# A decoder layer: another home for batch 1's x, another tile for batch 0's wkv, and new instruction lists

## The chip, the cores and the metric

The kernel runs on one core of a Trainium2 chip. A core has five engines with their own instruction streams: TensorE (PE, matmuls; PEld is its weight load), VectorE (DVE), ScalarE (ACT), GpSimd (POOL) and SyncE (SP), which here issues every DMA. Engines meet only at semaphores. The metric is the device time of one execution in microseconds, the median of several runs. All data is float32, 128 rows (partitions) at a time.

## What is computed

x and ctx are (4, 512, 512): four batches of 512 tokens with 512 channels. The reference, cut:

```python
x = x + attn(layernorm(x))
x = x + wkv2(w, u, k=layernorm(x), v=ctx)
x = x + ffn(layernorm(x))

def attn(x):                       # RWKV-4 time mix
    xs = x shifted by one token
    k, v, r = (x*tm + xs*(1-tm)) @ W.T     # three projections, each its own tm and W
    wkv = scan over tokens: (e1*aa + e2*v) / (e1*bb + e2), with a running maximum
    return (sigmoid(r) * layernorm(wkv) * g + b ...) @ Wo.T
def ffn(x):                        # 1408 inner channels
    return ((silu(x @ G.T * gs) * (x @ U.T * us)) @ Dn.T) * ds
```

wkv2 is a scan of the same kind without projections. Both scans run along the tokens and carry their state, channel by channel.

## The kernel before

Each batch passes through a row of steps. A step is a short piece of one engine's stream, named by kind, index and batch ("up6.0" is unit 6 of batch 0). The order in which an engine takes its steps is written out by hand in five lists of the file, PE_STEPS, ACT_STEPS, DVE_STEPS, POOL_STEPS and SP_STEPS; nothing else sets it, and every engine takes its own steps strictly in turn. Each step waits at semaphores for what it needs.

For one batch: x is loaded (xload), DVE takes its statistics (stat1), DVE and ACT normalise it (norm0, norm1), PE transposes it so that channels lie on partitions (turn1). ACT copies it scaled (share_k, share_v, share_r), DVE adds the shifted part (mixk, mixv, mixr), and PE projects (k, v, r: four units each of four 512-wide matmuls). The first scan is done by DVE and ACT per group of 128 channels: front, den, nv, num, part, fin; fin writes wkv. PE turns wkv back to tokens (turn2), its statistics are taken (stat2), it is normalised (norm2, norm3), turned again (return2), scaled and gated (rw, with the tanh of r), and projected (wo). x1 adds the first residual (loaded by rload into xres) and x's sums are taken for the next layernorm (sq on ACT, nb and rn on POOL, norm4, norm5). turn3, the second scan (xfront, xin, xden, xnum, xpart, xfin), y (turn back), xf (second residual), norm6, norm7, turn4_0 and turn4_1 (the two halves of the tokens), z4 (split in a high part z4h by ACT and a rest z4l by DVE). The FFN has 22 up units (sixteen 256-wide matmuls each, one 128-channel slice of one half of the tokens), for each a silu and a prod that make h, its split (high, rest), and 22 down units of four 512-wide matmuls. out writes the result.

The projections and the turns of all batches share four PSUM banks in turn: use n of a bank waits until use n-4 has been read (need_drained). The two slots of the scans are shared likewise. The FFN of batch b runs on PE beside the attention of batch b+1, which mostly DVE and ACT work on.

Tiles that matter here: mixv holds x of a batch from its load on, then v's mixed input. xres holds the first residual, xf the second. zt holds the transposed, normalised x; `wkv = zt` (L265) has the first scan write into it when x is no longer wanted. So share_k0 of batch b waits for turn2 of batch b-1 (L739), and load_x of batch 1 (L422) waits until the last nv of batch 0 has read v. load_res (L428) for batch 0 stands in the head of the SP stream, ahead of the FFN's weights. mixr of batch 0 is in z, of batch 1 in xf, then in mixk. There is a step kind "warm" (L638) for two 128x128 matmuls of the identity into a PSUM tile that nobody reads; the list before doesn't use it.

Of the kernel before, what the change touches and what calls it, by code (L numbers as in the profile page):

```python
# [44 lines left out]
def decoder_layer(nc, x, ctx_t, wk_t, wv_t, wr_t, wo_t, vecs_in, gate_t, up_t, down_t, ffn_scales, down_s, out):  # L45
# [21 lines left out]
    def steps(text):  # L67
# [8 lines left out]
        up15.0 up16.0 up17.0 down11.0 up18.0 r1.2 down12.0 down13.0 up19.0 down14.0 up20.0 up21.0
        down15.0 down16.0 down17.0 r2.2 down18.0 down19.0 down20.0 down21.0 y.1 r3.2 turn4_0.1 turn4_1.1
        up0.1 turn2.2 up1.1 up2.1 up3.1 return2.2 up4.1 down0.1 down1.1 turn1.3 up5.1 wo.2 k0.3 k1.3
        v0.3 v1.3 k2.3 k3.3 up6.1 up7.1 down2.1 v2.3 v3.3 down3.1 down4.1 up8.1 up9.1 turn3.2 down5.1
        up10.1 up11.1 down6.1 down7.1 up12.1 up13.1 down8.1 down9.1 down10.1 up14.1 up15.1 r0.3 up16.1  # L80
        up17.1 down11.1 r1.3 r2.3 r3.3 down12.1 up18.1 up19.1 down13.1 down14.1 down15.1 y.2 up20.1
        down16.1 down17.1 up21.1 down18.1 turn4_0.2 down19.1 down20.1 down21.1 up0.2 up1.2 up2.2 up3.2
        turn4_1.2 up4.2 turn2.3 up5.2 up6.2 down0.2 down1.2 return2.3 up7.2 wo.3 up8.2 up9.2 turn3.3
        down2.2 down3.2 up10.2 down4.2 down5.2 up11.2 down6.2 down7.2 up12.2 up13.2 down8.2 down9.2
        down10.2 up14.2 up15.2 up16.2 up17.2 down11.2 down12.2 down13.2 up18.2 down14.2 down15.2 up19.2
# [18 lines left out]
        share_v0.2 silu6.0 share_v1.2 share_v2.2 share_v3.2 sq4.1 norm4.1 sq5.1 norm5.1 front0.2
        front1.2 part0.2 share_r0.2 share_r1.2 silu7.0 part1.2 high2.0 high3.0 share_r2.2 front2.2
        silu8.0 silu9.0 front3.2 share_r3.2 silu10.0 silu11.0 part2.2 part3.2 high4.0 high5.0 silu12.0
        silu13.0 high6.0 xfront0.1 xfront1.1 silu14.0 silu15.0 tanh0.2 silu16.0 silu17.0 xpart0.1
        xpart1.1 xfront2.1 high7.0 silu18.0 high8.0 silu19.0 xfront3.1 silu20.0 silu21.0 xpart2.1
# [1016 lines left out]
```

## Time and profile before

| | us |
|---|---|
| median of 3 runs | 588.87 (588.06 to 589.04) |
| profiled execution | 589.12 |
| its span, first to last instruction | 587.2 |
| PE busy | 531.2 (90%) |
| DVE busy | 458.0 (78%) |
| ACT busy | 361.9 (62%) |
| mean granted clock of PE | 0.972 |

The profile is one execution. A timeline row gives the start in us, the length in us, the engine, the line of the kernel, the operation with out<-in, the shapes, the count of instructions merged in the row and, in brackets, how long the engine had been idle before it and what ended that.
### The profile page before, as it was taken

To read this page: it belongs to the slowest core of one execution; us is meant where nothing else is said; L and a number is where in the kernel's file an instruction comes from. 1 tells how busy PE (TensorE), PEld (TensorE's weight loads), DVE (VectorE), ACT (ScalarE), POOL (GpSimd) and SP (SyncE) were. 2 spreads that over 40 slices of the span, in tenths; PEclk is the share of its full clock that TensorE was granted. 3 is DMA by queue.
4 is the path that set the end of the run, shared out by engine and by line. 5 is a ranking of instruction groups with operands and counts; after the bars stand their busy time and mean duration, and the time that the engine had idled before them with its cause. 6 is when DMAs were issued, how large, how long until landed. Compare 5 with 4: busy or idle time off the path is not lost.

```text
span 587.2 us, 7506 instructions
## 1 busy us (share of the span) xinstructions
PE 531.2 (90%) x2658; PEld 379.4 (65%) x2658; DVE 458.0 (78%) x742; ACT 361.9 (62%) x559; POOL 51.0 (9%) x155
## 2 busy tenths in 40 slices
PE   1899388769589999999979999999999999999995
PEld 1444244324288447888658446985989588999995
DVE  4899878799987689999966699999867289853344
ACT  2828789655748458767757466887645377743321
POOL 2000300200222100000023110000101100101000
PEclk9999899889869999999999999999999999999999
DMA  8999800010220000010340000001120010000011
GB/s 308 413 300 390 326 0 0 2 36 0 76 104 2 0 1 0 2 37 1 116 136 1 0 1 0 2 31 60 55 73 2 0 37 28 9 19 19 1 37 38
DMA packets 14263, 39.08 MB, mean 67 GB/s; under 512 B 1232, under 2 KB 1232, under 8 KB 14032
## 3 DMA queue, kind: packets, MB, share of 16 engines
q1 hardware_dynamic: 14224, 38.57, 18.9%
q8 instruction: 23, 0.38, 0.3%
q14 instruction: 16, 0.13, 0.1%
HBM read 34.37 MB, written 12.85 MB: 80 GB/s over the span
## 4 chain that ended last, share of the span: by engine, by line
PE 62%; DVE 19%; ACT 7%; issue 7%; POOL 4%; DMA 1%; SPq 0%; POOLq 0%; DVEq 0%; ACTq 0%
PE gu L658 23%; PE bank L570 12%; PE dacc L584 12%; PE bank L632 9%; PE bank L559 5%; DVE t_slot L885 2%; ACT L681 2%; DVE t_slot L945 1%; DVE t_st L1023 1%; POOL t_rstd L532 1%; DVE t_stats L911 1%; DVE t_slot L966 1%; DVE t_stats L864 1%; DVE t_slot L949 1%; ACT t_mixk L712 1%
## 5 line engine op out<-in xcount | busy, mean ns | idle before, releaser
L658 PE MATMUL gu<-t_z4h,t_gate 128*128 128x256 f32 x352 | 91.9, 294 | 3.6 <-DVE t_h L1060 1.4
L658 PE MATMUL gu<-t_z4h,t_up 128*128 128x256 f32 x352 | 87.9, 283 | 0.0
L658 PE MATMUL gu<-t_z4l,t_up 128*128 128x256 f32 x352 | 87.9, 282 | 0.0
L658 PE MATMUL gu<-t_z4l,t_gate 128*128 128x256 f32 x352 | 87.8, 282 | 0.0
L810 ACT ACTIVATE t_h<-gu,t_fsc 128x256 f32<-128x256 f32 x88 | 40.7, 472 | 64.4 <-PE gu L658 55.2
L681 ACT ACT_TABLE_LOAD x60 | 77.0, 1283 | 1.8 <-PEq L1119 0.7
L1060 DVE SCALAR_TENSOR_TENSOR t_h<-gu,t_fsc,t_h 128x256 f32<-128x256 f32 x88 | 41.1, 478 | 40.2 <-ACT t_h L810 40.1
L658 PEld LDWEIGHTS gu<-t_z4h,t_gate 128*128 128x128 f32 x352 | 66.8, 190 | 8.2 <-DVE t_h L1060 3.0
L584 PE MATMUL dacc<-t_down,t_hh 128*128 128x512 f32 x176 | 71.1, 404 | 0.2
L584 PE MATMUL dacc<-t_down,t_hl 128*128 128x512 f32 x176 | 68.9, 391 | 0.0
L658 PEld LDWEIGHTS gu<-t_z4l,t_gate 128*128 128x128 f32 x352 | 66.9, 190 | 2.2 <-issue 1.4
L658 PEld LDWEIGHTS gu<-t_z4l,t_up 128*128 128x128 f32 x352 | 66.9, 190 | 0.0
L658 PEld LDWEIGHTS gu<-t_z4h,t_up 128*128 128x128 f32 x352 | 66.9, 190 | 0.0
L570 PE MATMUL bank<-t_mixk,t_wk 128*128 128x512 f32 x128 | 59.4, 614 | 3.0 <-DVE t_mixk L894 3.0
L570 PE MATMUL bank<-t_mixv,t_wv 128*128 128x512 f32 x128 | 56.8, 593 | 0.9 <-ACT t_z L784 0.9
L632 PE MATMUL bank<-t_wo,t_tanh_r 128*128 128x512 f32 x128 | 55.6, 592 | 0.0
L570 PEld LDWEIGHTS bank<-t_mixk,t_wk 128*128 128x128 f32 x128 | 24.7, 196 | 35.6 <-issue 30.0
L570 PEld LDWEIGHTS bank<-t_mixv,t_wv 128*128 128x128 f32 x128 | 24.2, 190 | 30.4 <-issue 28.9
L632 PEld LDWEIGHTS bank<-t_wo,t_tanh_r 128*128 128x128 f32 x128 | 24.1, 190 | 29.2 <-issue 27.5
L695 ACT ACTIVATE t_hh<-t_h 128x512 fp32r<-128x512 f32 x44 | 27.2, 625 | 21.4 <-PE dacc L584 11.6
L885 DVE TENSOR_TENSOR t_slot<-t_slot 128x1024 f32<-128x1024 f32 x32 | 39.0, 1218 | 0.7 <-ACT t_slot L797 0.7
L904 DVE TENSOR_TENSOR t_hl<-t_h,t_hh 128x512 fp32r<-128x512 f32 x44 | 29.7, 684 | 12.0 <-ACT t_hh L695 11.8
(128 smaller groups left out, 924.9 us busy)
## 6 DMA issues: line engine op xcount, KB each, us to landing
t_mixv<-in_x SPq DMA_DIRECT2D x8, 512.0 KB, 4.9
t_xres<-in_x SPq DMA_DIRECT2D x8, 512.0 KB, 4.4
t_ctxt<-in_ctx_t SPq DMA_DIRECT2D x16, 256.0 KB, 2.7
out<-t_otile SPq DMA_DIRECT2D x16, 256.0 KB, 2.4
...
```

The source lines that it names most:

```text
L532: pool.tensor_tensor(rstd[:, half(k)], veps[:, half(k)], small[:, MINUS_HALF, half(k)], ALU.pow).then_inc(rstd_done, 1)
L559: done = pe.transpose(bank_of(b, s, m)[:, k * P:(k + 1) * P], src[:, k, m * P:(m + 1) * P], ident[:, :])
L570: last = pe.matmul(bank_of(b, s, c)[:, :], w[:, k, c * P:(c + 1) * P], src[:, k, :], start=(k == 0), stop=(k == C - 1))
L584: last = pe.matmul(dacc[j][:, :], as_read(part[:, ring(b, u), j * P:(j + 1) * P], exact), as_read(down[:, i, :], exact), start=(i == 0 and ...
L632: done = pe.matmul(bank_of(b, s, m)[:, :], tanh_r[:, k, m * P:(m + 1) * P], wo[:, k, :], start=(k == 0), stop=(k == C - 1))
L658: last = pe.matmul(gu[u % 2][:, side, :], as_read(w[:, k, i * P:(i + 1) * P], exact), as_read(part[:, k, hf * HALF:(hf + 1) * HALF], exact ...
L681: act.preload_act_table_set(name)
L695: act.activation(pair(hh, b, p), pair(h, b, p), ACT.Copy).then_inc(hh_done, 1)
L810: act.activation(h[:, ring(b, u), :], gu[u % 2][:, 0, :], ACT.Silu, scale=fsc[:, 0, u % NI:u % NI + 1]).then_inc(silu_done, 1)
L885: dve.tensor_tensor(slot[:, c % 2, 2:4, :], both, slot[:, c % 2, 0:1, :].to_broadcast([P, 2, T]), ALU.mult).then_inc(square, 1)
L904: dve.tensor_tensor(pair(hl, b, p), pair(h, b, p), pair(hh, b, p).bitcast(F32), ALU.subtract).then_inc(hl_done, 1)
L1060: dve.scalar_tensor_tensor(out=h[:, ring(b, u), :], in0=gu[u % 2][:, 1, :], scalar=fsc[:, 1, u % NI:u % NI + 1], in1=h[:, ring(b, u), :], ...
```

## The change

1. x of batch 1 is loaded in the head of the program, where the first residual of batch 0 was loaded, into xf instead of mixv. Its statistics and the reads of norm0 and norm1 of batch 1 go to xf; they still write mixv, now after v of batch 0 is projected.
2. The first residual of batch 0 is loaded later, after turn2 of batch 0, since xres now holds wkv of batch 0 until then.
3. share_k0 waits for what still reads its target tiles, batch by batch, no longer always for turn2 of the batch before.
4. All five lists are new. PE's has 26 "warm" steps, all in batch 0.

```diff
-        wkv = zt
+        def wkv(b):
+            return xres if b == 0 else zt
+        def x_home(b):
+            return xf if b == 1 else mixv
...
             def load_x(b, hf):
-                need(sp, newv_done, b - 1, C)
-                sp.dma_start(mixv[:, hf * HB:(hf + 1) * HB, :], rows_of(b, hf)).then_inc(x_in[hf], 16)
+                if b > 1:
+                    need(sp, newv_done, b - 1, C)
+                sp.dma_start(x_home(b)[:, hf * HB:(hf + 1) * HB, :], rows_of(b, hf)).then_inc(x_in[hf], 16)
             def load_res(b, hf):
+                if b == 0:
+                    need_filled(sp, 0, "turn2", TB - 1)
                 need(sp, xf_done, b - 1, (hf + 1) * HB)
...
-            load_res(0, 0)
-            load_res(0, 1)
+            load_x(1, 0)
+            load_x(1, 1)
...
                     if c == 0:
-                        need(act, tanh_done, b - 1, C)
-                        need_before(act, b, "turn2", C - 1)
+                        if b > 0 and mixr(b - 1) is mixk:
+                            need(act, tanh_done, b - 1, C)
+                        elif b > 0:
+                            need_filled(act, b - 1, "k", C - 1)
+                        if b > 0 and wkv(b - 1) is zt:
+                            need_filled(act, b - 1, "turn2", C - 1)
+                        else:
+                            need(act, mix_done, b - 1, 3 * C)
...
     PE_STEPS = steps("""
-        turn1.0 k0.0 k1.0 v0.0 v1.0 k2.0 k3.0 r0.0 r1.0 v2.0 v3.0 r2.0 r3.0 turn2.0 turn1.1 k0.1 k1.1
+        warm0.0 warm1.0 warm2.0 warm3.0 warm4.0 warm5.0 turn1.0 warm6.0 warm7.0 warm8.0 k0.0 k1.0 v0.0
```

In DVE's list the steps of batch 0's scan are in another order in the head (front0.0 stands ahead of mixv3.0 and mixr0.0), rw0 to rw2 of batch 0 stand between front0.1 and mixv2.1, and stat1_0.1 and stat1_1.1 stand where they stood, behind stat2_0.0 and stat2_1.0.

PE, from turn2 of batch 0 (the second transposes that read t_zt or t_xres) to wo.0 (t_wo). Before, from turn2.0:

```order
L559 MATMUL bank<-t_ident,t_zt 128x128 x16
L559 MATMUL bank<-t_ident,t_mixv 128x128 x16
L570 MATMUL bank<-t_mixk,t_wk 128x512 x8
L570 MATMUL bank<-t_mixv,t_wv 128x512 x4
L559 MATMUL bank<-t_ident,t_z 128x128 x16
L570 MATMUL bank<-t_mixv,t_wv 128x512 x4
L632 MATMUL bank<-t_wo,t_tanh_r 128x512 x16
```

Now, from the two warm steps ahead of turn2.0 (gu<-t_ident):

```order
L650 MATMUL gu<-t_ident 128x128 x4
L568 MATMUL bank<-t_ident,t_xres 128x128 x16
L650 MATMUL gu<-t_ident 128x128 x4
L568 MATMUL bank<-t_ident,t_mixv 128x128 x16
L579 MATMUL bank<-t_mixk,t_wk 128x512 x4
L650 MATMUL gu<-t_ident 128x128 x12
L568 MATMUL bank<-t_ident,t_z 128x128 x16
L579 MATMUL bank<-t_mixk,t_wk 128x512 x4
L579 MATMUL bank<-t_mixv,t_wv 128x512 x8
L650 MATMUL gu<-t_ident 128x128 x2
L641 MATMUL bank<-t_wo,t_tanh_r 128x512 x16
```

return2.0 (the transposes of t_z) moved from behind k0.1, k1.1 and v0.1 to behind k0.1 alone, with six warm steps ahead of it; k1.1, v0.1 and v1.1 stand between it and wo.0, and two more warm steps stand ahead of turn1.1.

DVE, around batch 0's last layernorm, from part2.1 (before) and from xf_0.0 (now). t_xf,t_sums is xf, t_z4l is the rest part of the FFN's input, the pair on t_slot 128x1024 and t_zt is fin2.1, t_slot<-t_slot,t_st is part. Before:

```order
L977 TENSOR_TENSOR t_slot<-t_slot,t_st 128x2x512
L1048 SCALAR_TENSOR_TENSOR t_xf,t_sums<-bank,t_xres 128x512 x3
L1074 TENSOR_SCALAR t_general<-gu 1x1
L1048 SCALAR_TENSOR_TENSOR t_xf,t_sums<-bank,t_xres 128x512
L959 SCALAR_TENSOR_TENSOR t_st<-t_fade,t_slot 128x512
L972 SCALAR_TENSOR_TENSOR t_st<-t_fade,t_slot 128x512
L877 TENSOR_SCALAR t_z<-t_xf,t_rstd,t_nmr 128x512
L977 TENSOR_TENSOR t_slot<-t_slot,t_st 128x2x512
L877 TENSOR_SCALAR t_z<-t_xf,t_rstd,t_nmr 128x512
L885 TENSOR_TENSOR t_slot<-t_slot 128x1024
L887 SCALAR_TENSOR_TENSOR t_zt<-t_slot 128x512
L1055 TENSOR_TENSOR t_z4l<-bank,t_z4h 128x2x256 x4
```

Now:

```order
L1067 SCALAR_TENSOR_TENSOR t_xf,t_sums<-bank,t_xres 128x512 x4
L1086 TENSOR_REDUCE t_inexact<-t_low_sums 128x1
L996 TENSOR_TENSOR t_slot<-t_slot,t_st 128x2x512
L978 SCALAR_TENSOR_TENSOR t_st<-t_fade,t_slot 128x512
L1093 TENSOR_SCALAR t_general<-gu 1x1
L894 TENSOR_SCALAR t_z<-t_xf,t_rstd,t_nmr 128x512
L991 SCALAR_TENSOR_TENSOR t_st<-t_fade,t_slot 128x512
L894 TENSOR_SCALAR t_z<-t_xf,t_rstd,t_nmr 128x512
L996 TENSOR_TENSOR t_slot<-t_slot,t_st 128x2x512
L1074 TENSOR_TENSOR t_z4l<-bank,t_z4h 128x2x256 x2
L902 TENSOR_TENSOR t_slot<-t_slot 128x1024
L904 SCALAR_TENSOR_TENSOR t_zt<-t_slot 128x512
```

The first half of z4l moved ahead of fin2.1 and behind part3.1; part2.1 stands behind xf, where before it stood ahead of xf.

PE, around y.1 (bank<-t_ident,t_z 128x128 behind the last down unit of batch 0); t_wr with t_mixk is r3.2. Before:

```order
L584 MATMUL dacc<-t_down,t_hh 128x512
L584 MATMUL dacc<-t_down,t_hl 128x512
L559 MATMUL bank<-t_ident,t_z 128x128 x16
L570 MATMUL bank<-t_mixk,t_wr 128x512 x4
L609 MATMUL bank<-t_ident,t_z 128x128 x16
L658 MATMUL gu<-t_z4h,t_gate 128x256
```

Now:

```order
L593 MATMUL dacc<-t_down,t_hh 128x512
L593 MATMUL dacc<-t_down,t_hl 128x512
L568 MATMUL bank<-t_ident,t_z 128x128 x16
L618 MATMUL bank<-t_ident,t_z 128x128 x16
L667 MATMUL gu<-t_z4h,t_gate 128x256
L667 MATMUL gu<-t_z4l,t_gate 128x256
```

r3.2 stands no longer between y.1 and turn4 of batch 1; it moved ahead of the last four down units of batch 0.

## Rows read from the trace of the kernel before

**Rows 1.** Windows of all engines: length, busy (instructions) by engine, clock, DMA, GB/s
```profile
0.00:167.10 167.10, 123.45 (x339) 61.30 (x339) 141.75 (x223) 111.38 (x161) 17.25 (x55) 0.92 0.48 172
167.10:188.30 21.20, 21.02 (x161) 20.79 (x162) 16.69 (x39) 13.29 (x23) 5.55 (x16) 0.89 0.01 2
202.00:292.70 90.70, 90.44 (x449) 64.65 (x447) 84.61 (x116) 64.84 (x91) 1.62 (x7) 1.00 0.08 24
292.70:302.50 9.80, 6.12 (x25) 3.17 (x25) 6.07 (x15) 6.95 (x15) 2.93 (x10) 1.00 0.71 215
302.50:581.40 278.90, 276.45 (x1656) 223.45 (x1656) 198.44 (x334) 158.61 (x258) 22.45 (x64) 1.00 0.06 20
```

**Rows 2.** Windows of PE alone: length, busy, granted clock, DMA
```profile
68.00:70.00 2.00, 0.00 (x0) 0.79 1.06 389
76.00:78.00 2.00, 0.70 (x2) 1.00 0.00 0
126.00:128.00 2.00, 0.00 (x0) 0.80 0.00 0
156.00:158.00 2.00, 0.00 (x0) 0.98 0.23 10
170.00:172.00 2.00, 2.00 (x13) 0.61 0.00 0
```

**Rows 3.** Windows of DVE alone
```profile
16.00:63.30 47.30, 45.21 (x56) 1.00 1.01 371
```

**Rows 4.** Timeline of PE, 10 to 64 us: start, us, line, operation
```profile
53.69 7.03 PE L570 MATMUL bank<-t_z,t_wr 128*128 128x512 f32 x16
62.90 1.31 PE L559 MATMUL bank<-t_ident,t_zt 128*128 128x128 f32 x10 [1.85 <-ACT t_tanh_r L759]
```

**Rows 5.** Part 6 of the page, the loads of x
```profile
t_mixv<-in_x SPq DMA_DIRECT2D x8, 512.0 KB, 4.9
```

**Rows 6.** Timeline of the DMA queue
```profile
56.04 1.08 SPq L426 DMA_DIRECT2D t_mixv<-in_x  x2
```

**Rows 7.** Timeline of all engines, 60 to 77 us
```profile
64.25 1.29 DVE L864 BATCH_NORM_STATS2 t_stats<-bank 128x6 f32<-128x512 f32 x2 [1.01 <-PE bank L559]
67.21 1.25 DVE L911 BATCH_NORM_STATS2 t_stats<-t_mixv 128x6 f32<-128x512 f32 x2
72.13 3.67 PE L559 MATMUL bank<-t_ident,t_mixv 128*128 128x128 f32 x16 [7.59 <-DVE t_mixv L919]
```

**Rows 8.** Timeline of PE, 76 to 99 us
```profile
77.30 7.66 PE L570 MATMUL bank<-t_mixk,t_wk 128*128 128x512 f32 x16 [1.50 <-DVE t_mixk L894]
89.91 1.64 PE L559 MATMUL bank<-t_ident,t_z 128*128 128x128 f32 x13 [1.18 <-DVE t_slot L966]
95.95 3.60 PE L632 MATMUL bank<-t_wo,t_tanh_r 128*128 128x512 f32 x8
```

**Rows 9.** Timeline of DVE, 107 to 186 us
```profile
154.32 1.23 DVE L977 TENSOR_TENSOR t_slot<-t_slot,t_st 128x1024 f32<-128x1024 f32 x1
163.81 1.22 DVE L885 TENSOR_TENSOR t_slot<-t_slot 128x1024 f32<-128x1024 f32 x1
165.67 2.47 DVE L1055 TENSOR_TENSOR t_z4l<-bank,t_z4h 128x512 fp32r<-128x512 f32 x4
```

**Rows 10.** Timeline of PE, 110 to 168 us
```profile
129.37 2.93 PE L570 MATMUL bank<-t_xf,t_wr 128*128 128x512 f32 x3 [5.17 <-DVE t_slot L1005]
162.18 3.74 PE L609 MATMUL bank<-t_ident,t_z 128*128 128x128 f32 x16 [7.23 <-DVE t_z L877]
167.10 0.55 PE L658 MATMUL gu<-t_z4h,t_gate 128*128 128x256 f32 x1 [1.18 <-DVE t_z4l L1055]
```

**Rows 11.** Timeline of PE, 278 to 306 us
```profile
291.04 1.64 PE L559 MATMUL bank<-t_ident,t_z 128*128 128x128 f32 x13 [0.19 <-ACT t_tanh_r L759]
293.21 3.70 PE L570 MATMUL bank<-t_mixk,t_wr 128*128 128x512 f32 x8 [0.53 <-DVE t_xf L1048]
298.63 1.40 PE L609 MATMUL bank<-t_ident,t_z 128*128 128x128 f32 x8 [1.72 <-DVE t_z L877]
```

More of the change, by code:

```diff
@@ L76, in decoder_layer @@
[L76 to L85, printed above, removed]
@@ new lines, in decoder_layer @@
+        v1.0 k2.0 k3.0 v2.0 v3.0 r0.0 r1.0 r2.0 r3.0 warm9.0 warm10.0 turn2.0 warm17.0 warm18.0 turn1.1
+        k0.1 warm11.0 warm12.0 warm13.0 warm14.0 warm15.0 warm16.0 return2.0 k1.1 v0.1 v1.1 warm19.0
+        wo.0 warm20.0 warm21.0 turn3.0 r0.1 r1.1 r2.1 r3.1 k2.1 k3.1 v2.1 v3.1 warm22.0 warm23.0 y.0
+        flag.0 warm24.0 warm25.0 turn4_0.0 turn4_1.0 up0.0 up1.0 turn2.1 up2.0 up3.0 up4.0 down0.0
+        return2.1 up5.0 down1.0 up6.0 turn1.2 up7.0 wo.1 k0.2 k1.2 v0.2 k2.2 k3.2 up8.0 up9.0 v1.2 v2.2
@@ new lines, in decoder_layer @@
+        up10.0 down2.0 up11.0 down3.0 down4.0 down5.0 v3.2 down6.0 down7.0 down8.0 down9.0 up12.0 up13.0
+        turn3.1 up14.0 down10.0 up15.0 r0.2 up16.0 r1.2 down11.0 up17.0 down12.0 down13.0 up18.0 up19.0
+        down14.0 down15.0 down16.0 down17.0 up20.0 up21.0 r2.2 r3.2 down18.0 down19.0 down20.0 down21.0
+        y.1 turn4_0.1 turn4_1.1 up0.1 turn2.2 up1.1 up2.1 up3.1 return2.2 down0.1 down1.1 up4.1 turn1.3
+        up5.1 wo.2 k0.3 k1.3 v0.3 v1.3 k2.3 k3.3 v2.3 up6.1 up7.1 down2.1 down3.1 down4.1 down5.1 v3.3
@@ L104, in decoder_layer @@
[L104 to L108, printed above, removed]
@@ L130, in decoder_layer @@
         stat1_0.0 stat1_1.0 norm0.0 norm1.0 mixk0.0 mixk1.0 mixk2.0 mixk3.0 mixv0.0 mixv1.0 mixv2.0
-        mixv3.0 mixr0.0 front0.0 front1.0 mixr1.0 den0.0 nv0.0 mixr2.0 num0.0 nv1.0 part0.0 den1.0
-        num1.0 part1.0 fin0.0 mixr3.0 fin1.0 front2.0 front3.0 den2.0 nv2.0 num2.0 part2.0 nv3.0 den3.0
-        num3.0 part3.0 fin2.0 fin3.0 stat2_0.0 stat2_1.0 stat1_0.1 stat1_1.1 norm2.0 norm3.0 norm0.1
-        norm1.1 mixk0.1 mixk1.1 mixk2.1 mixk3.1 mixv0.1 mixv1.1 mixv2.1 mixv3.1 front0.1 front1.1 nv0.1
@@ new lines, in decoder_layer @@
+        part3.0 fin2.0 fin3.0 stat2_0.0 stat2_1.0 stat1_0.1 stat1_1.1 norm2.0 norm3.0 norm0.1 norm1.1
+        mixk0.1 mixk1.1 mixk2.1 mixk3.1 mixv0.1 mixv1.1 front0.1 rw0.0 rw1.0 rw2.0 mixv2.1 mixv3.1 rw3.0
+        mixr0.1 front1.1 nv0.1 den0.1 nv1.1 num0.1 part0.1 den1.1 num1.1 mixr1.1 part1.1 x1_0.0 x1_1.0
+        x1_2.0 fin0.1 x1_3.0 norm4.0 fin1.1 norm5.0 mixr2.1 mixr3.1 xfront0.0 xfront1.0 xin0.0 xin1.0
+        xden0.0 xnum0.0 xpart0.0 xden1.0 xnum1.0 xpart1.0 xfin0.0 xfront2.0 xfin1.0 xin2.0 xfront3.0
@@ new lines, in decoder_layer @@
+        mixk2.2 prod6.0 prod7.0 x1_3.1 mixk3.2 mixv0.2 mixv1.2 mixv2.2 mixv3.2 front0.2 front1.2 den0.2
+        nv0.2 num0.2 part0.2 norm4.1 norm5.1 den1.2 mixr0.2 mixr1.2 mixr2.2 fin0.2 prod8.0 front2.2
+        nv1.2 num1.2 part1.2 prod9.0 nv2.2 fin1.2 front3.2 den2.2 rest3.0 rest4.0 num2.2 part2.2
+        prod10.0 prod11.0 nv3.2 rest5.0 den3.2 num3.2 part3.2 prod12.0 prod13.0 fin2.2 mixr3.2 fin3.2
+        xfront0.1 rest6.0 out0.0 xfront1.1 xin0.1 prod14.0 prod15.0 xden0.1 xnum0.1 xpart0.1 xin1.1
@@ new lines, in decoder_layer @@
+        rw3.2 x1_0.2 mixk1.3 mixk2.3 mixk3.3 mixv0.3 mixv1.3 mixv2.3 mixv3.3 rest1.1 x1_1.2 x1_2.2
+        front0.3 prod4.1 x1_3.2 front1.3 den0.3 nv0.3 num0.3 prod5.1 part0.3 den1.3 norm4.2 norm5.2
+        nv1.3 rest2.1 num1.3 part1.3 mixr0.3 fin0.3 mixr1.3 fin1.3 front2.3 front3.3 den2.3 prod6.1
+        prod7.1 nv2.3 num2.3 nv3.3 prod8.1 part2.3 prod9.1 rest3.1 den3.3 num3.3 prod10.1 prod11.1
+        part3.3 rest4.1 mixr2.3 fin2.3 mixr3.3 fin3.3 xfront0.2 rest5.1 prod12.1 prod13.1 xfront1.2
```

168 lines of the change are left out of this document (84 added, 84 removed).

## Prediction

> **What bounds the kernel now.** I read the windows of all engines first, then the clock of TensorE (PE) where it waits, then the timelines around the waits.
>
> The windows cut the span in two parts [rows 1]. Up to 167.10 us, where the first FFN unit starts (up0.0), PE is busy 123.45 us of 167.10 and VectorE (DVE) 141.75: this part is a chain, mostly of DVE work, in which PE waits and in places runs slowly (mean granted clock 0.92). From 167.10 on PE is the bound: 21.02 of 21.20, 90.44 of 90.70 and, at the end, 276.45 of 278.90 us busy. Between these lies one hole, 292.70 to 302.50, where PE is busy 6.12 of 9.80 us: batch 1's second residual, its layernorm and turn4 have to pass before up0.1 can run. The reader is to see two rules in this. Before 167 us a shorter chain is a gain; after it, a PE unit taken out of the hole and put in front of it costs its full length.
>
> Where PE waits, its granted clock falls to the lower of its two levels. After the wait before turn1.1 it fell at about 69.2 us (0.79 is the mean of 68 to 70) and was back by 76.0; after the others it fell at about 127.2, then at about 157.9, and in this last case returned only at about 171.6 (0.61 over 170 to 172 is 1.56 us at half) [rows 2]. The waits were 7.59, 5.17 and 7.23 us [rows 7, 10]; 1.85 us of waiting before turn2.0 cost no clock [rows 4].
>
> **The change part by part.** My milestones are the start of wo.0, of up0.0, the end of y.1, the start of up0.1, and the end.
>
> The early load of x. Before, x of batch 1 is issued at 56.04 us and takes 4.9 us to land, some 61 us [rows 5, 6]. Its first reader, stat1_0.1, starts at 67.21 [rows 7], right behind stat2 of batch 0, and the new list of DVE leaves it there. The load was hidden, so its move is worth 0. It takes the place of the first residual's load, of the same size; that residual now waits for turn2.0 (some 64 us) and is wanted by x1_0.0 only after wo.0 has begun, at 95.95 [rows 8], over 30 us later: 0, and 4.9 us could go wrong without harm. wkv in the other tile costs the same writes and reads: 0. It frees zt for batch 1, but PE still has turn2.0 ahead of turn1.1, so nothing is released by it.
>
> The head, to batch 0's stats. DVE is busy 45.21 of 47.30 us from 16.0 to 63.3 [rows 3]; the new list holds the same operations, so at most 2.1 us go and at least 0. Putting front0.0 ahead of mixv3.0 and mixr0.0 and spreading the waits should take about half of it. The tanh on ScalarE (ACT) that frees the last bank of turn2.0 (the 1.85 us wait of rows 4) comes about as much earlier. I take -1.0 us for the stats at 64.25 and, with them, turn1.1 at 72.13 [rows 7].
>
> The warm-up matmuls. 26 steps of two 128x128 matmuls go into the waits of batch 0. Four matmuls of 128x512 take 7.03 - 3.60 = 3.43 us (x16 against x8) [rows 4, 8], so one takes 0.86, a 128-wide one a quarter of that, 0.21 us, and a step of two 0.43 us at full clock and 0.86 at half. They lie in waits except six steps behind k0.1 (2.6 us) and one before wo.0 (0.4 us). The two steps ahead of turn1.1 run at once behind turn2.0; over 6 us of waiting remain, near the three waits that did lose the clock, so turn1.1 and the start of k0.1 run at half. Before, the clock came back at 76.0, ahead of k0.1 at 77.30 [rows 2, 8]. After other restarts it took longer: from r2.1 at 129.37 about 4.7 us, from turn4 at 162.18 about 9.4 us [rows 2, 10]. I take 4.7 from k0.1's start (77.30 - 1.0 = 76.3): 4.7 us at half do 2.35 of its 3.43, the other 1.1 run at full, and it ends at 82.1. Before it took 7.66 - 3.60 = 4.06 us, paced by its inputs [rows 8], which would end it at 80.4. The ends are 0 and +3.4 us (all of k0.1 slow); I take +1.7.
>
> wo.0. PE goes on in a row: six warm-ups 2.6, return2.0 1.8, k1.1, v0.1 and v1.1 10.3, a warm-up 0.4: 82.1 + 15.1 = 97.2, against 95.95 [rows 8]. So +1.25 us, from -0.5 to +2.9. What waits behind it is x1, the layernorm and xfront0.0. Before, return2.0 stood later, at 89.91, after a wait of 1.18 us [rows 8]; the six warm-ups now sit where it would otherwise start.
>
> From wo.0 to up0.0. DVE is saturated in most of it. One partial sum (part2.1, at 154.32, 1.23 us) goes from ahead of batch 0's xf to behind it [rows 9]; the warm-ups behind wo.0 may shorten turn3.0 by some 0.4. So xf is at 1.25 - 1.2 - 0.4, about -0.3. Then the new list puts z4l of the first half ahead of fin2.1, which took 163.81 to 165.67 [rows 9]. up0.0 waited for it 1.18 us after turn4, which ended at 162.18 + 3.74 = 165.92 [rows 10]. Now it can start as turn4 ends, so at most 1.18 us go; part3.1 lands ahead of z4l, so I take 0.9 and get **up0.0 at -1.2 us**, 165.9; ends -3.0 and +0.8.
>
> From up0.0 to y.1. PE does the same units as before plus one: r3.2 stood behind y.1 (293.21, 3.70 us with its drain) [rows 11] and now stands ahead of it, 3.43 us. PE had no room for it: its idle time in 167.10 to 188.30 and in 202 to 292.70 is 0.18 and 0.26 us [rows 1]. I count +3.43, less these 0.44: +3.0, and y.1 ends at 292.68 - 1.2 + 3.0 = 294.5. The ends are +2.5 and +5 (the other moves of ups and downs, each of which must find its h ready).
>
> From y.1 to up0.1. This is a chain of DVE, ACT and POOL, 9.8 us before [rows 1], and I leave it at that. What r3.2 hid there is now an idle PE: from 292.68 to 298.63 is 5.95 us [rows 11], between the waits of 5.17 and 7.59 that lost the clock. There is no warm-up step in it. In batch 0 the low clock reached 4.46 us past up0.0's start (171.56 - 167.10), which is 2.2 us lost [rows 2, 10]. That row is the nearest case: +2.2, ends 0 and 3.4.
>
> The Trainium skill (TensorE: Matmul & The Clock Gate, "What's actually happening") says that the gate's monitor is free-running and not reset by the kernel's start. It would make each of these clock terms differ from run to run by its phase; the executions before, 588.06 to 589.04, are compatible with that and show no more.
>
> After up0.1 the same 159 PE steps follow in a slightly different order over 278.90 us with 2.45 us idle [rows 1]: 0, ends -2.4 and +2.4.
>
> **Sum.** -1.2 + 3.0 + 0 + 2.2 + 0 = +4.0 us on the profiled execution's 589.12, 593.1. That execution stood 0.25 above the median of 588.87, so 592.9.
>
> **The rivals.**
> The clock is held. If the warm-ups keep PE at its upper level through batch 0, k0.1 is 1.7 us earlier and turn4 and up0.0 lose nothing (2.2 us less): 592.9 - 3.9 = 589.0, no change. For it: 26 steps, two of them just ahead of turn4. Against: the waits are longer than the pairs. If the clock also stays up behind y.1, 2.2 more go and the kernel is **faster**, 586.8. It decides where the granted clock between 155 and 172 us, and between 294 and 310, stands at the lower level for less than about 1 us.
>
> The FFN of batch 0 finds its inputs late. PE has no slack after 167, so each wait that the moved downs, k3.2 and v2.2 make adds itself; two waits of 1.5 us give 595.9. For it: DVE too is nearly full there (84.61 of 90.70 us) [rows 1]. Against: only small moves.
>
> The change does nothing of weight: x's load was hidden, and 3.0 us ahead of y.1 could be met by a head better than I think (up0.0 at -3.0 instead of -1.2) and the 2.45 us of late idle time. That gives 592.9 - 1.8 - 2.2 = 588.9 as well.
>
> **How the numbers follow.** The forecast (591.0 to 594.6) gets 0.46, the late inputs 0.12, the held clock without the second stretch 0.12, with it 0.16, the last rival 0.09, the rest 0.05 to either side. 0.2% (1.2 us) is about what a measurement of this kernel can tell from no change. The two cases at 589 (0.21) I split 0.07 faster, 0.12 same, 0.02 slower. So faster 0.07 + 0.16 + 0.02 = 0.25, same 0.13, slower 0.62. The range 586.5 to 595.8 leaves out less than one in ten on either side; the forecast's own is 591.0 to 594.6.
>
> **What would show it.** In the changed profile: wo.0's first matmul near 97, up0.0 near 166, y.1 ending near 294.5, up0.1 near 304; between y.1 and turn4_0.1 no PE work for about 6 us, and a granted clock at half for a stretch that begins there; from up0.1 to PE's last matmul 279 to 281 us. The prediction is wrong if y.1 ends before 292.7, if up0.0 stands before 164, or if the clock stays up behind y.1.

## The result, and the profile after

The changed kernel takes 592.84 us (median of 4 executions, 592.11 to 593.17) against 588.87: the ratio is 1.0062, with a 95% interval of 1.0041 to 1.0083. It is slower by some 4 us. The forecast was 592.9 us. The profiled execution took 593.17 us, with a span of 591.4 us and a mean granted clock of 0.964.

The windows of all engines of the changed kernel, cut at the same events as [rows 1] (columns as there):

```profile
0.00:167.90 167.90, 135.46 (x442) 74.73 (x442) 139.74 (x220) 103.95 (x154) 18.52 (x55) 0.90 0.48 171
167.90:191.10 23.20, 23.04 (x184) 22.65 (x185) 18.82 (x42) 14.40 (x25) 5.15 (x16) 0.97 0.01 2
204.80:294.70 89.90, 89.86 (x433) 62.97 (x431) 86.48 (x119) 64.50 (x90) 4.27 (x8) 1.00 0.09 27
294.70:304.50 9.80, 3.73 (x17) 3.19 (x17) 5.95 (x14) 6.08 (x14) 2.92 (x10) 0.73 0.61 188
304.50:585.50 281.00, 277.19 (x1656) 223.69 (x1656) 198.83 (x333) 153.07 (x255) 20.61 (x64) 1.00 0.06 20
```

Three things are to be seen against [rows 1]. The hole between y.1 and up0.1 is again 9.80 us long, but PE is busy 3.73 us in it and no longer 6.12: r3.2 has gone from it. The last stretch has the same 1656 PE instructions, but PE idles 3.81 us in it, where it idled 2.45. And the mean clock ahead of up0.0 is 0.90, not 0.92, in spite of the warm steps.

The timeline of PE in the changed kernel, in the head, around y.1 and around y.2 (start and length in us, line; L568 turns, L579 projects, L618 is turn4, L667 an up unit, L593 a down unit, L641 wo):

```profile
71.28 3.68 PE L568 MATMUL bank<-t_ident,t_mixv 128*128 128x128 f32 x16 [6.70 <-DVE t_mixv L938]
76.46 5.81 PE L579 MATMUL bank<-t_mixk,t_wk 128*128 128x512 f32 x8 [1.50 <-DVE t_mixk L911]
84.78 1.91 PE L568 MATMUL bank<-t_ident,t_z 128*128 128x128 f32 x16
87.56 3.70 PE L579 MATMUL bank<-t_mixk,t_wk 128*128 128x512 f32 x8 [0.87 <-ACT t_z L801]
98.41 1.88 PE L641 MATMUL bank<-t_wo,t_tanh_r 128*128 128x512 f32 x4
...
163.94 3.68 PE L618 MATMUL bank<-t_ident,t_z 128*128 128x128 f32 x16 [2.85 <-DVE t_z L894]
168.06 0.55 PE L667 MATMUL gu<-t_z4h,t_gate 128*128 128x256 f32 x1 [0.45 <-DVE t_z4l L1074]
...
282.23 7.03 PE L579 MATMUL bank<-t_mixk,t_wr 128*128 128x512 f32 x16
292.76 1.91 PE L568 MATMUL bank<-t_ident,t_z 128*128 128x128 f32 x16
300.62 3.71 PE L618 MATMUL bank<-t_ident,t_z 128*128 128x128 f32 x16 [5.96 <-DVE t_z L894]
304.48 0.55 PE L667 MATMUL gu<-t_z4h,t_gate 128*128 128x256 f32 x1
...
423.97 0.66 PE L568 MATMUL bank<-t_ident,t_z 128*128 128x128 f32 x4 [0.50 <-DVE t_z L904]
425.83 0.66 PE L568 MATMUL bank<-t_ident,t_z 128*128 128x128 f32 x4 [1.20 <-DVE t_z L904]
432.52 1.09 PE L618 MATMUL bank<-t_ident,t_z 128*128 128x128 f32 x8 [0.47 <-DVE t_z L894]
```

These rows answer to [rows 7, 8, 10 and 11]. wo.0 stands at 98.41 (before 95.95), up0.0 at 168.06 (167.10), y.1 ends at 292.76 + 1.91 = 294.67 (292.68), up0.1 stands at 304.48 (302.49). The last three rows are y.2 and turn4_0.2; their waits, 2.17 us in all, have no counterpart before.

The granted clock of PE in the changed kernel (2 us each: busy, clock, DMA):

```profile
68.00:70.00 2.00, 0.00 (x0) 0.50 1.03 380
168.00:170.00 2.00, 1.94 (x11) 0.62 0.05 12
304.00:306.00 2.00, 1.85 (x9) 0.50 0.06 17
306.00:308.00 2.00, 2.00 (x19) 0.99 0.00 0
```

It is at the lower level up to about 169.5 us behind up0.0, 1.5 us of running at half where [rows 2] had 4.46; and up to 306.0 behind up0.1, 1.5 us again, where before it was never low.

**An account that adds up.** For each profile I cut the time from up0.0 on in three: up0.0 to the end of y.1 (the middle), the hole up to up0.1, and up0.1 to PE's last matmul (the late stretch). From the middle and the late stretch I take off what the clock cost: PE's busy time times (1 - granted clock), summed over windows of 1 us. What is left, the net length, repeats within 0.4 us between profiles whose lists are the same there; the clock's part differs from execution to execution. The last row of the table is the sum for this pair of profiles.

| us | up0.0 | middle, net | clock | hole | late, net | clock | last matmul |
|---|---|---|---|---|---|---|---|
| before | 167.10 | 123.35 | 2.23 | 9.81 | 278.85 | 0.00 | 581.34 |
| changed | 168.06 | 125.88 | 0.73 | 9.81 | 280.35 | 0.78 | 585.61 |
| difference | +0.96 | +2.53 | -1.50 | 0 | +1.50 | +0.78 | +4.27 |

### The profile page after: what moved, and what is told of

Its sections match the earlier page's. It is cut to its first block, busy times and chain, and to the rows that moved or that the text cites. A ratio compares the mean times of both kernels' runs of the same rounds, so it can differ in the third digit from the quotient of the medians.

```text
span 591.4 us, 7709 instructions
## 1 busy us (share of the span) xinstructions
PE 543.1 (92%) x2762; PEld 393.3 (67%) x2762; DVE 458.3 (77%) x742; ACT 350.2 (59%) x551; POOL 51.8 (9%) x155
## 4 chain that ended last, share of the span: by engine, by line
PE 83%; DVE 8%; ACT 3%; issue 3%; POOL 2%; DMA 1%; SPq 0%; POOLq 0%; DVEq 0%; ACTq 0%
PE gu L667 27%; PE bank L579 26%; PE dacc L593 13%; PE bank L641 9%; PE bank L568 6%; PE bank L618 1%; ACT L690 1%; DVE t_stats L928 1%; DVE t_otile L1100 1%; PE gu L650 1%; DMA t_vecs<-in_vecs 1%; DVE t_slot L902 1%; DVE t_st L1042 1%; DVE t_z L894 1%; DVE t_xf L1067 1%
## 5 line engine op out<-in xcount | busy, mean ns | idle before, releaser
L667 PE MATMUL gu<-t_z4h,t_gate 128*128 128x256 f32 x352 | 92.9, 297 | 1.3 <-DVE t_h L1079 0.7
L667 PE MATMUL gu<-t_z4l,t_gate 128*128 128x256 f32 x352 | 88.2, 283 | 0.0
L667 PE MATMUL gu<-t_z4l,t_up 128*128 128x256 f32 x352 | 87.3, 281 | 0.0
L667 PE MATMUL gu<-t_z4h,t_up 128*128 128x256 f32 x352 | 87.2, 281 | 0.0
L667 PEld LDWEIGHTS gu<-t_z4h,t_gate 128*128 128x128 f32 x352 | 67.3, 191 | 6.7 <-issue 3.2
L593 PE MATMUL dacc<-t_down,t_hh 128*128 128x512 f32 x176 | 71.0, 403 | 0.8 <-DVE t_otile L1100 0.7
L593 PE MATMUL dacc<-t_down,t_hl 128*128 128x512 f32 x176 | 68.9, 391 | 0.0
L667 PEld LDWEIGHTS gu<-t_z4l,t_gate 128*128 128x128 f32 x352 | 67.2, 191 | 2.5 <-issue 1.7
L667 PEld LDWEIGHTS gu<-t_z4h,t_up 128*128 128x128 f32 x352 | 66.4, 189 | 0.0
L667 PEld LDWEIGHTS gu<-t_z4l,t_up 128*128 128x128 f32 x352 | 66.3, 188 | 0.0
L579 PE MATMUL bank<-t_mixk,t_wk 128*128 128x512 f32 x128 | 59.3, 615 | 2.4 <-DVE t_mixk L911 1.5
L579 PE MATMUL bank<-t_mixv,t_wv 128*128 128x512 f32 x128 | 56.6, 592 | 0.0
L641 PE MATMUL bank<-t_wo,t_tanh_r 128*128 128x512 f32 x128 | 55.6, 592 | 0.0
L579 PEld LDWEIGHTS bank<-t_mixk,t_wk 128*128 128x128 f32 x128 | 24.6, 196 | 34.3 <-issue 28.1
L579 PEld LDWEIGHTS bank<-t_mixv,t_wv 128*128 128x128 f32 x128 | 24.2, 190 | 29.3 <-issue 28.9
L641 PEld LDWEIGHTS bank<-t_wo,t_tanh_r 128*128 128x128 f32 x128 | 24.0, 190 | 28.7 <-issue 27.7
```

Source lines behind the costliest of these rows:

```text
L579: last = pe.matmul(bank_of(b, s, c)[:, :], w[:, k, c * P:(c + 1) * P], src[:, k, :], start=(k == 0), stop=(k == C - 1))
L593: last = pe.matmul(dacc[j][:, :], as_read(part[:, ring(b, u), j * P:(j + 1) * P], exact), as_read(down[:, i, :], exact), start=(i == 0 and ...
L641: done = pe.matmul(bank_of(b, s, m)[:, :], tanh_r[:, k, m * P:(m + 1) * P], wo[:, k, :], start=(k == 0), stop=(k == C - 1))
L667: last = pe.matmul(gu[u % 2][:, side, :], as_read(w[:, k, i * P:(i + 1) * P], exact), as_read(part[:, k, hf * HALF:(hf + 1) * HALF], exact ...
```

## The experiments

Each has its own comparison with the kernel before on the same chip. Lists are cut at up0.0 and up0.1 (on ACT at silu0.0 and silu0.1, on DVE at prod0.0 and prod0.1) into head, middle and late.

### 1. The new code under the old lists

```diff
-SP: copy2.0 words1.0 xload0.1 xload1.1 words2.0 ctx2.0
+SP: copy2.0 words1.0 words2.0 rload0.0 rload1.0 ctx2.0
 PE, ACT, DVE, POOL: the lists of before
```

> The new code (x of batch 1 early, wkv of batch 0 in the other tile, the later load of the first residual) with the step lists of the kernel before. Theory: the load was hidden, so 588.9 us, within 1.2 of the kernel before. Rival (the tiles or the moved loads cost something by themselves): more than 590.1.

Measured: 589.23 against 588.76 us, ratio 1.0010 (0.9995 to 1.0025). The other homes of x and of wkv, the earlier load and share_k's other waits are worth nothing that can be measured (at most 1.5 us by the interval). The 4 us, or all but a small part of them, lie in the lists.

### 2. The new head alone

```diff
-PE, ACT, DVE up to up0.0: the lists of before
+PE, ACT, DVE up to up0.0: the lists of the changed kernel, warm steps included
```

> As the run with the new code alone, but the PE, ACT and DVE lists up to the first FFN unit (up0.0, silu0.0, prod0.0) are those of the changed kernel, warm-up steps included; everything behind is as before. Theory from the two traces: up0.0 comes 1.0 us later, but the low clock ends 1.5 us instead of 4.5 us behind it, so 588.4 to 589.9, no change. Rival (the head is what costs): 591 or more.

Measured: 589.76, ratio 1.0019 (1.0005 to 1.0033). In the profile up0.0 stands at 166.28, 0.8 earlier than before. But the old lists behind it then wait: PE idles 1.33 us in the middle (before 0.41), of it 0.27 and 0.66 at turn2.1, whose input DVE now writes behind z4l. Net middle 124.97.

### 3. The new middle alone

```diff
-PE, ACT, DVE from up0.0 to up0.1; POOL; SP: the lists of before
+PE, ACT, DVE from up0.0 to up0.1; POOL; SP: the lists of the changed kernel
```

> As the run with the new code alone, but the lists between up0.0 and up0.1 (with the POOL and SP lists) are those of the changed kernel, r3.2 ahead of y.1 among them. Theory: r3.2 costs its 3.4 us less some 0.3 of waits, and the low clock behind y.1 0.8 to 2.2 us: 592 to 594. Rival (r3.2 is met by slack elsewhere and the loss is in the other parts): 590.1 or less.

Measured: 594.26, ratio 1.0097 (1.0075 to 1.0120), more than the whole change. The net middle is 125.70. The rest is an artifact of the mixture, seen in the timeline of PE:

```profile
475.30 1.09 PE L566 MATMUL bank<-t_ident,t_z 128*128 128x128 f32 x8 [1.32 <-DVE t_z L892]
477.58 1.09 PE L566 MATMUL bank<-t_ident,t_z 128*128 128x128 f32 x8 [1.19 <-DVE t_z L892]
```

POOL's new order has nb5.3 ahead of rn4.3; under the old late lists nb5.3's input comes late, and batch 3's layernorm with it: 2.5 us. Experiment 9 repeats the middle without that.

### 4. The new late stretch alone

```diff
-PE, ACT, DVE from up0.1 on: the lists of before
+PE, ACT, DVE from up0.1 on: the lists of the changed kernel
```

> As the run with the new code alone, but the lists from up0.1 on are those of the changed kernel. Theory: in the trace of the changed kernel PE was idle 3.8 us of this stretch against 2.45 before, so +1.4 us: 590.2. Rival (that idle time belongs to what comes before it): 588.9.

Measured: 591.77, ratio 1.0044 (1.0026 to 1.0062). The net late stretch is 280.25, as in the changed kernel, with PE idle for 3.85 us. The prediction had 0 for it. And r3.2 stands behind y.1 here, yet the clock fell (windows of PE):

```profile
300.00:310.00 10.00, 9.39 (x56) 0.66 0.02 7
```

That cost 2.6 us in this execution. So r3.2 in the hole does not protect the clock. The median is 1.6 us above the 590.2 expected, and the clock goes with that: the seven executions with a mean granted clock of 0.971 to 0.977 have a median of 590.38 us, the five with 0.964 to 0.966 one of 593.19.

### 5. r3.2 put back behind y.1

```diff
-PE: r2.2 r3.2 down18.0 down19.0 down20.0 down21.0 y.1 turn4_0.1
+PE: r2.2 down18.0 down19.0 down20.0 down21.0 y.1 r3.2 turn4_0.1
-ACT: tanh3.2 sq6.1 sq7.1
+ACT: sq6.1 sq7.1 tanh3.2
```

> The changed kernel with one PE step moved: r3.2 stands behind y.1 again, as in the kernel before, and its tanh on ACT behind sq7.1. Theory (r3.2 ahead of y.1 costs its full length, behind y.1 it lies in a wait): y.1 ends about 3.4 us earlier, 291.2 in place of 294.7, y.1 to up0.1 stays 9.8 us, up0.1 near 301.1, and the time is about 3.4 us below the changed kernel's 592.8, near 589.4. If the clock also stays up behind y.1, another 0.8 us. Rival (the place of r3.2 is of no weight, since what is saved ahead of y.1 comes back as late waits of the last 280 us): 592 to 593, with up0.1 earlier by 3 us and PE idle behind up0.1 longer by as much.

Measured: 593.80 (591.26 to 594.34), ratio 1.0062 (1.0040 to 1.0083), the very ratio of the changed kernel. My theory of 3.4 us fell. The timeline of PE shows where they went:

```profile
286.53 0.47 PE L593 MATMUL dacc<-t_down,t_hh 128*128 128x512 f32 x1 [1.46 <-DVE t_hl L921]
293.89 3.70 PE L579 MATMUL bank<-t_mixk,t_wr 128*128 128x512 f32 x8 [0.90 <-DVE t_xf L1067]
```

and that of DVE, which has no gap from 284.50 to 292:

```profile
284.50 1.23 DVE L1042 TENSOR_TENSOR_SCAN t_st<-t_keep,t_slot 128x512 f32<-128x512 f32 x1
285.64 0.14 DVE L1045 COPY t_st<-t_slot 128x2 f32<-128x2 f32 x1
285.69 0.69 DVE L921 TENSOR_TENSOR t_hl<-t_h,t_hh 128x512 fp32r<-128x512 f32 x1
286.30 1.28 DVE L1050 SCALAR_TENSOR_TENSOR t_slot<-t_slot,t_beta,t_st 128x1024 f32<-128x1024 f32 x1
...
291.21 0.69 DVE L904 SCALAR_TENSOR_TENSOR t_z<-t_slot 128x512 f32<-128x512 f32 x1
```

PE, rid of r3.2, waits 1.46 us for the rest (t_hl) of h that down18.0 reads, which DVE writes behind a scan, and then for the z of y.1, written at 291.9. The net middle shrinks by 0.9 only, to 124.99; the hole is 0.4 us longer (10.17), which leaves a gain of 0.5 us, less than the intervals can tell. This profile also lost 2.60 us to the clock in its late stretch, the changed kernel's 0.78. In the new lists PE and DVE are both near full there (DVE 86.48 of 89.90 us), and r3.2 is partly the filling of waits.

### 6. r3.2 ahead of y.1 in the old lists

```diff
-PE: r2.2 down18.0 down19.0 down20.0 down21.0 y.1 r3.2 turn4_0.1
+PE: r2.2 r3.2 down18.0 down19.0 down20.0 down21.0 y.1 turn4_0.1
-ACT: sq6.1 sq7.1 tanh3.2
+ACT: tanh3.2 sq6.1 sq7.1
```

> The kernel before with one PE step moved: r3.2 stands behind r2.2, far ahead of y.1, and its tanh on ACT ahead of sq6.1. Theory: y.1 ends 3.0 to 3.4 us later, up0.1 likewise, and the time is 588.9 + 3.2 = 592.1; with a low clock behind y.1 that r3.2 no longer covers, up to 2 us more (594). Rival (PE's order there costs nothing by itself, it was the other new steps of the middle that cost): 588.9 to 589.5.

Measured: 591.70, ratio 1.0039 (1.0023 to 1.0054), 2.2 us slower. Net middle 126.25 against 123.35, +2.9, near its length of 3.43 us less the 0.4 of idle time (of which 0.2 is still there); hole 9.81 and net late stretch 278.83 unchanged; the clock cost nothing behind up0.1. In the old lists, where DVE is less late, the step does cost its length.

### 7. The changed kernel without warm steps

```diff
-PE: warm0.0 ... warm25.0 (26 steps)
```

> The changed kernel without its 26 warm steps. Theory (too short to hold the clock; where they stand behind k0.1 they cost their length): behind k0.1 six steps of 0.43 us go and one ahead of wo.0, so wo.0 stands up to 3 us earlier, less what return2.0 and k1.1 wait for their inputs; some of it is DVE's chain and doesn't come through: up0.0 at 0 to -1.5 us and a time of 591.3 to 592.8. Rival (the warm steps hold the clock in part of batch 0): the clock is at half for longer at k0.1 and around turn4_0.0, up0.0 1 to 2 us later, a time of 594 to 595.

Measured: 592.12, ratio 1.0051 (1.0032 to 1.0069), 0.7 us below the changed kernel if anything; the intervals overlap. In the profile wo.0 stands at 96.84 (98.41) and up0.0 at 166.55 (168.06). The timeline of PE from k0.1 to k1.1:

```profile
76.38 5.51 PE L577 MATMUL bank<-t_mixk,t_wk 128*128 128x512 f32 x8 [1.81 <-DVE t_mixk L909]
81.72 0.49 PE L566 MATMUL bank<-t_ident,t_z 128*128 128x128 f32 x3
83.92 1.64 PE L566 MATMUL bank<-t_ident,t_z 128*128 128x128 f32 x13 [1.71 <-DVE t_slot L966]
86.43 3.70 PE L577 MATMUL bank<-t_mixk,t_wk 128*128 128x512 f32 x8 [0.87 <-ACT t_z L799]
```

They don't hold the clock: with them turn1.1 takes 3.67 to 3.68 us (changed, experiments 2, 5 and 12), without them 3.30, where 16 transposes at the upper level take 1.91. k0.1's length is a draw: 5.81, 4.23, 5.06 and 4.23 us in those four profiles, 5.51 here. From k0.1's end to wo.0 it is 16.14 to 16.15 us in all four, and 14.95 without the steps: there they cost 1.2 us. Of the six behind k0.1 (2.6 us), 1.7 us lay in a wait of return2.0 for its input; k1.1 comes 1.1 us earlier without them.

### 8. The long waits filled

```diff
-PE: turn2.0 turn1.1 ... r1.1 r2.1 ... y.0 turn4_0.0
+PE: turn2.0 (14 warm) turn1.1 ... r1.1 (9 warm) r2.1 ... y.0 (14 warm) turn4_0.0
```

(in the kernel before)

> The kernel before with 37 warm steps that fill the three long waits of batch 0 nearly whole: 14 ahead of turn1.1 (6.0 of 7.59 us), 9 ahead of r2.1 (3.9 of 5.17), 14 ahead of turn4_0.0 (6.0 of 7.23). Theory (the clock falls where PE waits for 5 us and more; work that fills the wait keeps it up): granted clock 1.00 from 20 to 290 us, r2.1 1.2 us shorter at least, turn4_0.0 1.8 us in place of 3.7, no slow stretch behind up0.0 (2.2 us): up0.0 about 2 to 3 us earlier, and the time 588.9 - 4 = 585 (at most 0.5 us back where the warm steps overrun the wait). Rival (the low clock lies off the path, since DVE sets most of it, or the clock falls all the same): 588 to 589.

Measured: 589.18, ratio 0.9998 (0.9985 to 1.0011): no change, and yet the clock did what the theory wanted. The windows of PE at the places of [rows 2] where it had fallen:

```profile
68.00:70.00 2.00, 2.00 (x20) 1.00 1.05 386
128.00:130.00 2.00, 2.00 (x20) 1.00 0.03 8
156.00:158.00 2.00, 2.00 (x20) 1.00 0.00 0
168.00:170.00 2.00, 2.00 (x20) 1.00 0.02 4
```

turn4 of batch 0 takes two pieces of 1.09 us where it took 3.74. But the timeline of PE shows what its speed is worth:

```profile
162.54 1.09 PE L613 MATMUL bank<-t_ident,t_z 128*128 128x128 f32 x8 [0.98 <-DVE t_z L881]
164.31 1.09 PE L613 MATMUL bank<-t_ident,t_z 128*128 128x128 f32 x8 [0.68 <-DVE t_z L881]
167.46 0.36 PE L662 MATMUL gu<-t_z4h,t_gate 128*128 128x256 f32 x1 [2.05 <-DVE t_z4l L1059]
```

up0.0 now waits 2.05 us for z4l, behind fin2.1 on DVE, and stands where it stands with the old head unfilled (167.48 in the mean of seven profiles). In the old head the low clock ahead of up0.0 lies off the path.

### 9. The new middle again, with POOL and SP as before

```diff
-POOL: nb4.3 nb5.3 rn4.3 rn5.3
+POOL: nb4.3 rn4.3 nb5.3 rn5.3
```

(against experiment 3; nb5.1 likewise behind rn4.1, and SP as in experiment 1)

> The new lists of PE, ACT and DVE from up0.0 to up0.1 alone, with POOL and SP in the order of before (the run with the middle alone had the new POOL order under the late lists of before). Theory: the 2.5 us of PE waiting near 475 us go; apart from the clock up0.0 to the end of y.1 takes 125.8 us against 123.4 with the lists of before, up0.1 to the end 278.8, so the time is 588.9 + 2.5 = 591.4. Rival (the middle itself costs what that run showed): 593.5 or more.

Measured: 591.91, ratio 1.0050 (1.0037 to 1.0063), +2.9 us. Net middle 125.95, net late stretch 278.47; the 2.5 us at 475 are gone. The middle of the new lists costs about 2.5 us and no more.

### 10. The changed kernel with the old head

```diff
-PE, ACT, DVE up to up0.0: the lists of the changed kernel
+PE, ACT, DVE up to up0.0: the lists of before, no warm steps
```

> The changed kernel with the lists of before up to up0.0, without warm steps, and the new lists from there on: its distance from the changed kernel is what the new head is worth. Theory (the new head gains only some 0.3 us at up0.0 in the profiles so far, against 1.2 forecast): up0.0 near 167.6, and a time of 593.1, the same as the changed kernel. Rival (the new head loses 1 us, as the run with the head alone measured): 591.8. Rival (it gains the 1.2 us forecast): 594.0.

Measured: 593.61, ratio 1.0075 (1.0061 to 1.0088), 0.8 us above the changed kernel, with overlapping intervals. In its profile up0.0 is at 167.44 and the wait ahead of turn4 7.23 us again; the clock then costs 2.21 us behind up0.0.

### 11. Filled waits and DVE's new order together

```diff
-DVE: part2.1 xf_0.0 xf_1.0 xf_2.0 flag.0 xf_3.0 den3.1 num3.1 norm6.0 part3.1 norm7.0 fin2.1 z4_0_0.0
+DVE: xf_0.0 xf_1.0 xf_2.0 xf_3.0 part2.1 den3.1 flag.0 norm6.0 num3.1 norm7.0 part3.1 z4_0_0.0 z4_0_1.0 fin2.1
-PE: (14 warm) turn4_0.0 turn4_1.0 up0.0 turn2.1 up1.0
+PE: (12 warm) turn4_0.0 turn4_1.0 up0.0 up1.0 turn2.1
```

(against experiment 8; part2.1 and part3.1 on ACT likewise, and on DVE prod1.0 ahead of stat2_1.1)

> The kernel before with its long waits of batch 0 filled by warm steps (35 of them), and besides the order of the changed kernel on DVE and ACT from xf of batch 0 to prod0.0: part2.1 behind xf, the first half of z4l ahead of fin2.1; up1.0 ahead of turn2.1 on PE. Filling alone moved nothing, since up0.0 then waited 2.05 us for z4l. Theory (DVE's order sets up0.0 once the clock is held): up0.0 waits under 0.6 us and stands 1.2 to 2.4 us earlier than 167.46, and the time is 589.2 - 1.5 = 587.7. Rival (what is gained at up0.0 is lost again at turn2.1 and y.1, since DVE has the same work in the middle): 589 to 590.

Measured: 591.10, ratio 1.0040 (1.0024 to 1.0055), slower. up0.0 stands at 166.32, 1.1 us earlier than in experiment 8, and behind it the timeline of PE shows

```profile
171.09 1.20 PE L562 MATMUL bank<-t_ident,t_zt 128*128 128x128 f32 x9 [0.27 <-DVE t_z4l L1058]
172.95 0.66 PE L562 MATMUL bank<-t_ident,t_zt 128*128 128x128 f32 x4 [0.66 <-DVE t_zt L890]
179.22 1.75 PE L562 MATMUL bank<-t_ident,t_z 128*128 128x128 f32 x14 [1.22 <-DVE t_z L880]
```

PE idles 2.90 us in the middle and the net middle is 127.33, 3.8 more than in experiment 8. An early up0.0 is not a gain by itself: DVE carries batch 1's scan across it, and what is put off there is paid for in the middle.

### 12. Feeding y.2's wait

```diff
-PE: down18.1 down19.1 y.2 down20.1 down21.1 r2.3 turn4_0.2 r3.3 up0.2
+PE: down18.1 down19.1 down20.1 down21.1 y.2 r2.3 r3.3 turn4_0.2 up0.2
```

(in the changed kernel)

> The changed kernel with five PE steps in another order in the last 280 us: down20.1 and down21.1 stand ahead of y.2 and r3.3 ahead of turn4_0.2. Theory (the 1.4 us more that PE idles behind up0.1 are the waits of y.2 for the second scan, 0.50 and 1.20 us, and 0.47 ahead of turn4_0.2): PE's idle time behind up0.1 falls from 3.8 to about 2.2 us, the stretch from up0.1 to the end from 280.4 to about 279 us apart from the clock, and the time from 592.8 to about 591.3. Rival (DVE is as late at the next place, so that the wait only moves): the stretch stays at 280.3 us or more and the time at 592 to 593.

Measured: 601.42, ratio 1.0223 (1.0210 to 1.0237), 8.6 us above the changed kernel: my edit was a bad one. PE and DVE in the timeline:

```profile
425.63 0.47 PE L593 MATMUL dacc<-t_down,t_hh 128*128 128x512 f32 x1 [3.94 <-DVE t_hl L921]
441.48 0.36 PE L667 MATMUL gu<-t_z4h,t_gate 128*128 128x256 f32 x1 [1.84 <-ACT t_z4h L821]
...
424.80 0.69 DVE L921 TENSOR_TENSOR t_hl<-t_h,t_hh 128x512 fp32r<-128x512 f32 x1
430.88 0.69 DVE L1067 SCALAR_TENSOR_TENSOR t_xf<-bank,t_xres 128x512 f32<-128x512 f32 x1 [5.40 <-PE bank L568]
```

DVE writes the rest that down20.1 reads only behind both z of y.2. So the downs could not fill the wait; they stood in it for 3.94 us, with y.2 behind them, and DVE in turn waited 5.40 us for y.2. PE idles 9.31 us in the late stretch. The theory that the waits of y.2 make the late stretch longer isn't refuted (both are in the trace, and experiment 4 has them too), but this experiment doesn't show that they can be removed.

## Why the prediction was right, and where it was right by luck

The total came out within 0.1 us of the median. Its mechanism, a PE step put ahead of y.1 where PE has no room, holds; but three of its terms were wrong (up0.0, the clock behind y.1 and the late stretch), and their errors made up for each other. That part of the agreement is luck.

**The early load and the other tile: 0.** Right as far as experiment 1 can tell: ratio 1.0010, with an interval up to 1.0025.

**Head and k0.1.** turn1.1 came 0.85 earlier (forecast 1.0), and k0.1 ended at 82.27 (forecast 82.1), partly at half clock as forecast. wo.0 came at 98.41, forecast 97.2. What I had left out: k1.1 waits 0.87 us for ACT to read the bank that return2.0 filled, after return2.0 has just been delayed; the remaining 0.3 are drains and starts of steps. The 98.41 is also a draw, by k0.1's clock: over the four profiles with the new head and its warm steps wo.0 stands at 96.81 to 98.41 (mean 97.68), over the seven with the old head unfilled at 95.77 to 96.91 (mean 96.31). That is a shift of +1.4, against +1.25 forecast.

**up0.0.** Forecast -1.2, measured +0.96 in the one profile. The seven profiles with the old head unfilled put up0.0 at 166.94 to 168.07 (mean 167.48), the four with the new one and its warm steps at 166.28 to 168.42 (mean 167.59): the true shift is near 0. The step that failed is the account from wo.0 to up0.0. It was 71.15 us before and is 69.65 in the changed kernel, -1.50 (-1.4 to -1.7 in experiments 2, 5 and 7, near 0 in experiment 12), where the prediction's terms for it (1.2 for part2.1, 0.4 for turn3.0, 0.9 for z4l) make -2.45 against wo.0. The wait for z4l did shrink, from 1.18 to 0.45 us. But the first xf came only 0.8 us nearer to wo.0, not 1.6 (the timelines of DVE, before and changed):

```profile
155.46 0.68 DVE L1048 SCALAR_TENSOR_TENSOR t_xf<-bank,t_xres 128x512 f32<-128x512 f32 x1
...
157.14 0.69 DVE L1067 SCALAR_TENSOR_TENSOR t_xf<-bank,t_xres 128x512 f32<-128x512 f32 x1 [0.37 <-PE bank L568]
```

With part2.1 out of the way, DVE waits 0.37 us for the bank of y.0 on PE; so it does in every profile with the new head. The warm steps too lie on this path: by experiment 7 they put wo.0 back by 1.2 us.

**The middle.** Forecast +3.0. Net of the clock it is +2.53, and 125.69 to 126.03 in the six profiles with the new middle lists and r3.2 in them, against 123.34 to 123.53 in the four with the old lists behind the old head (before, experiments 1, 4 and 8). That the cause is r3.2's length is shown for the old lists (experiment 6, +2.9). For the new lists it is only part: putting it back (experiment 5) gains 0.9 us of net middle, since DVE is then the later one; the other 1.6 us come from other moves in the middle, and no run says which. The row of DVE's load, 84.61 of 90.70 us in [rows 1], was read in the prediction as a reason for one rival and not for this term.

**The clock behind y.1: forecast +2.2, and this is the term that failed as a mechanism.** I had said that r3.2's place decides. The clock did fall there, at about 299.2 us, and stayed low 1.5 us past up0.1: 0.78 us. But the cost behind up0.1 was 0.78, 0, 0, 0.18, 1.04 and 0 with r3.2 ahead of y.1 (changed, experiments 3, 6, 7, 9, 10; 12 is left out, since its own long wait cost clock too), and 0, 0.68, 0, 2.62, 2.60, 0.86 and 0 with it behind (before, experiments 1, 2, 4, 5, 8, 11). These profiles show no effect of its place, and the same hole of 9.8 us costs between 0 and 2.6 us.

**The clock behind up0.0** I had left at the 2.2 us of [rows 2]; it was 0.73. Behind the old head, its wait of 7.23 us (6.68 in experiment 6) unbroken, it cost 2.23, 0, 2.34, 1.86, 0, 0 and 2.21 (mean 1.2; before, experiments 1, 3, 4, 6, 9, 10). Behind the new one, where the flag and the warm steps break the wait, it cost 0.73, 0.54, 0.42 and 0 (changed, experiments 2, 5, 12), with the flag alone 0 (experiment 7), and filled up 0 and 0 (experiments 8, 11). So the breaking of the wait may be worth some 0.8 us on average, which agrees with the 0.8 us of experiment 10. Experiment 8 speaks against it: filled up, the kernel before kept its clock behind up0.0 and its time didn't move (-0.9 to +0.6 us by the interval). It stays open.

**The late stretch.** Forecast 0, measured +1.50 net, and in every profile with the new late lists (280.24 to 280.45, against 278.47 to 278.85; experiments 3 and 12 apart, which have waits of their own there). The waits of y.2 and turn4_0.2, 2.17 us in the rows above, less some 0.6 that other waits shrank, make it. I had counted the same 159 steps and not asked, as I did at y.1, whether their inputs come in time.

The sum of the terms as measured over all profiles is about 0 + 2.5 + 1.5 and some tenths from the clock in either direction: 4.0, as forecast, but with the late lists in the place of the clock.
